# Halving the sixteen weights once, and picking a row's weight on GpSimd instead of ScalarE

## The reference, cut to what matters

```python
# x: (128 rows, 128 channels, 2048 steps); weights: (16, 128, 128)
W = weights[itok_B_0_15]                          # one of 16 matrices for each row
x = x + einsum('bct,bcd->bdt', x, W)              # stage 1, per row b
mask = arange(2048) < itok_B_8_3872[:, None]
u = x * mask[:, None, :]
k = S4D kernel of (log_dt, C, log_A_real, A_imag) # one filter of 2048 taps for each channel
y = irfft(rfft(u) * rfft(k))[..., :2048] + u * D  # causal convolution, per channel h
x = x + y * mask[:, None, :]                      # stage 2
```

## Time and profile before

| what | value |
|---|---|
| median of 3 runs | 2327.47 us (2319.9 to 2331.1) |
| the profiled execution | 2328.0 us, its span 2326.2 us |
| busy, share of the span | PE 93%, PEld 81%, DVE 71%, ACT 64%, POOL 51% |
| DMA | 716.26 MB, 308 GB/s over the span |
| granted TensorE clock | 0.993 of full speed |

### The profile page before, as it was taken

One profiled execution on the slowest core, in us unless ns is written; L12 is line 12 of the kernel. 1 busy time (PEld: TensorE's weight loads), 2 busy tenths in 40 slices (PEclk: granted clock), 3 DMA queues, 4 the chain that ended last, 5 costly groups with the idle time before them and its releaser, 6 DMA issues.

```text
span 2326.2 us, 61624 instructions
## 1 busy us (share of the span) xinstructions
PE 2169.9 (93%) x15101; PEld 1882.4 (81%) x15101; DVE 1652.8 (71%) x3359; ACT 1478.4 (64%) x4354; POOL 1175.6 (51%) x1862
## 2 busy tenths in 40 slices
PE   5777878999999999999999999999999999999999
PEld 2222226888888888888888888889999999999999
DVE  4999304777777777777777777667777777777776
ACT  4556556777777777777777677545555555555555
POOL 0995503666666666666666666433333333333332
PEclk9999999999999999999999999999999999999999
DMA  8999999999999999999999999889999899989997
GB/s 313 415 410 396 399 357 332 311 321 326 315 310 313 327 315 323 318 317 319 315 317 326 304 312 318 256 247 268 274 277 268 267 269 273 272 264 274 272 275 230
DMA packets 337444, 716.26 MB, mean 308 GB/s; under 512 B 39554, under 2 KB 170884, under 8 KB 337412
## 3 DMA queue, kind: packets, MB, share of 16 engines
q1 hardware_dynamic: 282116, 514.54, 72.5%
q10 hardware_dynamic: 55296, 201.35, 21.7%
HBM read 395.92 MB, written 319.82 MB: 308 GB/s over the span
## 4 chain that ended last, share of the span: by engine, by line
PE 52%; DMA 18%; SPq 8%; issue 7%; DVE 6%; ACT 5%; ACTq 5%; DVEq 0%
PE bank L907 11%; DMA toep<-k_scratch 11%; PE bank L908 10%; PE bank L909 10%; PE bank L952 6%; PE bank L944 6%; PE bank L889 5%; PE bank L876 3%; DMA row_x<-in_x 3%; SPq L339 3%; DVE decay L810 3%; SPq L355 2%; ACTq L522 2%; ACT row_y L547 2%; DMA decay<-x_scratch 2%
## 5 line engine op out<-in xcount | busy, mean ns | idle before, releaser
L798 DVE TENSOR_TENSOR u_lo<-bank,u_hi 128x512 fp32r<-128x512 f32 x512 | 352.2, 688 | 212.6 <-ACT u_hi L604 209.0
L907 PE MATMUL bank<-t_hi,u_hi 128*128 128x256 f32 x1024 | 361.8, 353 | 40.3 <-DMA toep<-k_scratch 39.4
L952 PE MATMUL bank<-toep,u_odd 128*128 128x128 f32 x2048 | 393.2, 273 | 0.0
L810 DVE COPY_PREDICATED decay<-mask,bank 128x512 f32<-128x512 uint8 x512 | 379.3, 741 | 14.0 <-PE bank L909 4.3
L547 ACT ACTIVATE row_y<-bank 128x512 f32<-128x512 f32 x512 | 301.6, 589 | 133.5 <-ACT row_y L547 47.5
L490 POOL TENSOR_TENSOR x_lo<-row_x,x_hi 128x256 fp32r<-128x256 f32 x496 | 371.5, 779 | 0.0
L804 DVE TENSOR_TENSOR s_lo<-state,s_hi 128x128 fp32r<-128x128 f32 x768 | 238.0, 310 | 163.5 <-ACT s_hi L616 160.5
L876 PE MATMUL bank<-row_x,w_sel 128*128 128x512 f32 x528 | 266.1, 631 | 90.9 <-DMA row_x<-in_x 51.3
L467 POOL TENSOR_TENSOR outer<-par 128x256 f32<-128x256 f32 x512 | 315.3, 637 | 20.5
L464 POOL COPY par<-table 128x71 f32 (+1 forms) x256 | 62.3, 243 | 514.1 <-PE bank L909 514.1
L613 ACT ACTIVATE state<-bank 128x128 f32<-128x128 f32 x768 | 211.4, 275 | 168.4 <-PE bank L909 150.5
(11 more groups left out here) (139 smaller groups left out, 5437.7 us busy)
## 6 DMA issues: line engine op xcount, KB each, us to landing
row_x<-in_x SPq DMA_DIRECT2D x256, 512.0 KB, 6.6
x_scratch<-row_y ACTq DMA_DIRECT2D x256, 512.0 KB, 5.7
decay<-x_scratch SPq DMA_DIRECT2D x256, 512.0 KB, 5.9
out<-decay SPq DMA_DIRECT2D x128, 512.0 KB, 4.7
out<-decay ACTq DMA_DIRECT2D x128, 512.0 KB, 5.6
b_scratch<-b_mat SPq DMA_DIRECT2D x128, 256.0 KB, 6.5
t_hi<-k_scratch SPq DMA_DIRECT2D x256, 128.0 KB, 4.8
t_lo<-k_scratch SPq DMA_DIRECT2D x256, 128.0 KB, 4.6
```

Source lines behind the costliest of these rows:

```text
L798: v.tensor_tensor(u_lo[j % 2][:, blocks, :], t_bank[q][:, :].rearrange("s (k b) -> s k b", b=B), u_hi[j % 2][:, blocks, :].bitcast(fp32), ...
L810: v.copy_predicated(tile[j][:, cols], mask[:, seg * SEG + q * BANK:seg * SEG + (q + 1) * BANK], y_bank[q][:, :]).then_inc(y_taken, 1)
L907: mm(to, w_hi, m_hi, start=start, stop=False, skip_group_check=True)
L952: mm(y[:, P:CHUNK], u_odd[i][:, c, :], toep[j][:, P - 1::-1], start=False, stop=True, skip_group_check=True)
```

## The change

The sixteen weights (already with the identity added) are rounded once, by one ScalarE instruction over 128x2048, into a new tensor `w_all_hi`, at the place where `halve_w` of row 0 stood. `halve_w` is gone from ScalarE. In `split_row` GpSimd reads the row's condition into a register, waits for the buffer (`row_made`), copies the chosen rounded half to `w_hi`, forms `w_lo` from `w_all` and `w_all_hi`, and only then waits for `x_hi`. ScalarE's wait for the buffer moves into `halve_x`. The row stage is as before.

```diff
+        w_all_hi = sb("w_all_hi", [P, NCOND, P], fp32r)
+        w_halved = sem("w_halved")
...
             def split_row(m, j):
 
-                i = j % 2
+                i, n = j % 2, m + ROWS_FIRST
+                which = pool.value_load(cond_sb[0:1, bass.ds(n, 1)], min_val=0, max_val=NCOND - 1)
+                pool.wait_ge(row_made, n * NQ - NQ)
+                whole, half = (a[:, bass.ds(which, 1), :].rearrange("c k d -> c (k d)") for a in (w_all, w_all_hi))
+                pool.tensor_copy(w_hi[i][:, :], half)
+                pool.tensor_tensor(w_lo[i][:, :], whole, half.bitcast(fp32), ALU.subtract)
                 pool.wait_ge(row_halved, m + 1)
-                pool.tensor_tensor(w_lo[i][:, :], w_sel[j][:, :], w_hi[i][:, :].bitcast(fp32), ALU.subtract)
...
+            pool.wait_ge(w_halved, 1)
             for m in range(2):
                 split_row(m, m)
...
                 if q == 0:
+                    act.wait_ge(row_made, n * NQ - NQ)
                     act.wait_ge(x_loaded[j], n * 4 + (16 - j * 4))
...
-            def halve_w(m, j):
-
-                n = m + ROWS_FIRST
-                which = act.value_load(cond_sb[0:1, bass.ds(n, 1)], min_val=0, max_val=NCOND - 1)
-                act.wait_ge(row_made, n * NQ - NQ)
-                w = w_all[:, bass.ds(which, 1), :].rearrange("c k d -> c (k d)")
-                nc.scalar.activation(w_sel[j][:, :], w, ACT.Copy)
-                nc.scalar.activation(w_hi[j % 2][:, :], w, ACT.Copy)
...
-            halve_w(0, 0)
+            nc.scalar.activation(w_all_hi[:, :, :], w_all[:, :, :], ACT.Copy).then_inc(w_halved, 1)
...
                     if next_row:
-                        halve_w(k + 1, j1)
                         halve_x(k + 1, j1, 0)
```

## The result

The changed kernel takes 2318.84 us in the median of 12 runs (2307.13 to 2324.89), against 2326.35 us of before in the same rounds: ratio 0.9964, 95% interval 0.9949 to 0.998. In a second series it took 2322.24 us, ratio 0.9974 (0.9954 to 0.9994). So it is faster by some 0.3%, and both intervals leave out 1. That is less than the 0.5% that the prediction took as the limit of what one can tell; the forecast was 2324.0.

A forecast was written before the change was run, and what follows sets the result against it. The bound was two interleaved channel loops, each of TensorE's body, issue and the late Toeplitz load's transfer. The sum was 2328.0 - 5 + 1 + 0 = 2324.0 us, own range 2318 to 2328, overall range 2312 to 2335.

The forecast's parts named there:

- ScalarE's late state costs TensorE, and the change ends it: Interleaved segment: TensorE's 0.31 us wait for state, 50 times, goes; at 0.2 us each, 10 us of body.
- The end of the body follows TensorE, so VectorE's part costs nothing: End of a channel: take_y comes 0.29 us after TensorE's last product, so VectorE's handover counts nothing; 9 us at most.
- rival B: The whole loop shortens, by 7.8 us and 9 us of VectorE's handover, to 2311 us; chance 0.12.
- A saving in the body is worth half: Two interleaved loops, even and odd channels: a microsecond saved in one body gives half; 10 us becomes 5 us.
- 1 us is given back: Interleaved segment: TensorE may find the other loop's channel ahead and earlier issues partly queue; 1 us of the 5 lost.
- GpSimd's work is hidden: Per row, GpSimd's added read, copy and subtraction, 0.9 + 0.3 + 0.46 = 1.7 us, fit into 3.16 us of idle time.
- Once: nothing: Before the first row, ScalarE's one-time 128x2048 rounding takes 2.2 us and costs 0, at most 0.5 us.
- Rival A: Nothing arrives: DMA engines at 0.96 absorb the earlier issues, each Toeplitz load lands when it did; 2328 us, chance 0.16.
- Rival C: Slower by collision: SyncE's earlier store of the filter's rows meets the Toeplitz loads in flight; 2338 us, chance 0.09.
- Rival D: GpSimd is late: a read over 2.7 us delays x_lo and par; at 3.7 us, 2390 us; chance 0.03.

The follow-up runs named there:

- e1: The kernel before the change, with Toeplitz tiles loaded for the first four channels only: 2270.49 us, ratio 0.976 to the kernel before.
- e2: The changed kernel with Toeplitz tiles loaded for the first four channels only: 2237.19 us, ratio 0.9615 to the kernel before.
- e5: The kernel before the change run once more, word for word the same: 2324.33 us, ratio 0.999.
- e9: The changed kernel with SyncE's store of the matrices moved behind the Toeplitz loads of the same channel: 2366.47 us, ratio 1.0183 to the kernel before.
- e3: The kernel before the change, with Toeplitz loads issued ahead of the x_scratch load and the store of the matrices: 2482.46 us, ratio 1.0666.
- e4: The changed kernel with Toeplitz loads issued ahead of the x_scratch load and the store of the matrices: 2473.16 us, ratio 1.0634 to the kernel before.
- e11: The kernel before the change, with the matrices' store moved behind the Toeplitz loads and the row load behind the filter's store: 2338.91 us, ratio 1.0062.
- e10: The changed kernel with the matrices' store moved behind the Toeplitz loads and the row load behind the filter's store: 2283.40 us, ratio 0.9829.
- e7: The kernel before the change, with row loads of 64 of the 128 channels in the interleaved segment: 2313.24 us, ratio 0.9935.

## Why the prediction was right, point by point

- **ScalarE's late state costs TensorE, and the change ends it.** Right, and shown by e1 and e2 with the wait in the rows. The size of a case was a little too small: I took 0.2 us of the visible 0.31. In the channels behind a gap under 8.35 us, where nearly all of these waits are, TensorE's part went from 7.59 and 7.57 us to 7.31 in both profiles, 0.27 each. Over all channels it shortened by 0.09 us, or 12 us in sum, where the prediction had 10.
- **The end of the body follows TensorE, so VectorE's part costs nothing.** Wrong. This was read off 0.29 us between the last product and `take_y` in one channel, and in that channel VectorE came straight from `e_lo`. The handover was 0.20 us in the mean, 0.26 behind a short gap, and it fell to 0.15. That is 0.05 us, 6 us in sum and 3 on the segment, a third of the whole saving. The prediction costed it at nothing and kept up to 9 us for the range and for rival B.
- **A saving in the body is worth half.** The pieces add up to two channels in all four profiles. The body's 0.14 us are 17 us in sum, and half of that is 8.6 us.
- **1 us is given back.** Too little. About 3.7 us were: 8.6 less the 4.9 by the `x_hi` rows. The place was named (TensorE still at the other loop's channel) and is seen as 0.17 us more after the landing. The two errors, 3.6 us too little saved and 2.7 too little given back, nearly cancel; 4 us net were forecast and 4.9 were found in the segment. That the total came so close is luck, all the more as the pairs of profiles differ by 3.5 to 4.9 us within themselves. By the medians the changed kernel is 7.5 us below the kernel before in the first series, and in the second 5.8 below the kernel before (2328.07) and 2.1 below e5.
- **GpSimd's work is hidden.** Right. The read took 0.68 us where 0.9 was allowed, partly while `e_mat` still ran, the copy 0.29 for 0.3, the subtraction 0.47 for 0.46. `x_lo` still waits 2.1 us, and 1.8 was said.
- **Once: nothing.** Right; 1.93 us for 2.2.
- **Rival A** (nothing arrives because the DMA engines are full) falls by the two ratios that leave out 1. Its condition holds while the Toeplitz loads are in flight (a share of 0.99), and some of the saving was given back. **Rival B** (the whole loop shortens, by 17 us) named `e_lo`, and this became short. Both of its parts came, and both smaller: 5.8 us from TensorE's part for its 7.8, 3 from the handover for its 9. VectorE's groups from 600 to 1400 us (busy us, mean ns), before and then after:

```profile
L804 DVE TENSOR_TENSOR s_lo<-state,s_hi 128x128 fp32r<-128x128 f32 x269 | 82.5, 307 | 102.6 <-ACT s_hi L616 102.4
L793 DVE TENSOR_TENSOR e_lo<-e_mat,e_hi 128x256 fp32r<-128x256 f32 x90 | 73.0, 811 | 0.0
L762 DVE TENSOR_TENSOR m_mat<-halves,par 128x128 f32<-128x128 f32 x89 | 63.1, 709 | 0.0
```
```profile
L802 DVE TENSOR_TENSOR s_lo<-state,s_hi 128x128 fp32r<-128x128 f32 x269 | 113.5, 422 | 112.3 <-ACT s_hi L615 106.7
...
L791 DVE TENSOR_TENSOR e_lo<-e_mat,e_hi 128x256 fp32r<-128x256 f32 x90 | 40.5, 449 | 0.0
...
L760 DVE TENSOR_TENSOR m_mat<-halves,par 128x128 f32<-128x128 f32 x90 | 25.1, 279 | 0.0
```

`e_lo` fell from 811 to 449 ns and `m_mat` from 709 to 279, `s_lo` rose from 307 to 422. The longest `e_lo` of the whole span took 875 ns before and 455 after. The second `take_y` waits 0.53 us for TensorE after the change, so most of VectorE's time went into its own idle time, and the 0.05 us of handover are what reached the loop. How much of that is `e_lo`'s and how much comes from the earlier `u_hi` was not separated. The Trainium skill ("SBUF — State Buffer", Who interferes with whom) lets exactly these instructions, with two SBUF inputs, block against GpSimd's reads of SBUF. By it `s_lo`, which GpSimd's copy and subtraction may now meet, should rise, and it did; that this is the cause of all three was not tested by itself.
- **Rival C** (the filter's store collides with the loads) had its condition misread: it took the store to start a few tenths after the load's landing, and in the kernel before it is issued 2.9 us ahead of that landing in every channel. It did start earlier, 5.4 us after the body's start instead of 5.8, and the landing did not get longer (4.88 to 4.74). **Rival D** fell by the 2.1 us that are left.

The point that I had not seen is the Toeplitz load's own dependence on the filter's store. It was 5.3 us of SyncE's waits and became the bound as soon as the load was moved (e9, and with the wait for `x_scratch` e3 and e4).

## What to carry to other kernels

When a wait ends on two engines by turns, price a saving by taking the covering wait away altogether: 33 us showed here where the kernel as it stood gave 5. Before calling an instruction bound by the engine that feeds it, look at what its own engine did just before: 0.29 us behind TensorE was VectorE's `e_lo`, not TensorE. Before moving a transfer up in a queue, look for what it waits for that has only just been in time; moving that one first turned a loss of 1.8% into a gain of 1.7%. And read a small gain from two profiles of each kernel, by the stretch that was changed: the untouched row stage alone moved its end by up to 10 us.

## What the runs showed of the hardware

- A register read from SBUF has no fixed price: 277 ns at the least on ScalarE, 568 in the median before, 1077 in e11 and up to 1481; on GpSimd 358 at the least and 682 in the median in the changed kernel, 930 in e10. The longer ones came in the kernels whose loads were reordered. What lengthens the read was not isolated; a Toeplitz load in flight is at most a part of it (954 ns without one, 1120 with one, in e11).
- GpSimd's sequencer reads the register while its engine still works on `e_mat`: a read of 0.68 us left only 45.7 / 116 = 0.39 us of idle time.
- One 128x2048 rounding on ScalarE took 1.93 us. Sixteen 128x128 ones would take 3.3 us, an estimate from the 0.41 us in the earlier trace rows from the start of `w_sel` to that of `x_hi`, with `w_sel` and `w_hi` in between (16 x 0.41 / 2).
- A load's time to landing did not fall with traffic issued behind it: 256 KB less of that in each channel left it at 4.9 us (e7). It was 2.8 to 3.4 us where 1.0 to 1.4 MB stood ahead of it (e3, e4, e9), 4.8 us with 1.7 MB, and 4.8 and 5.2 us with 2.1 MB (e11, e10). The amount ahead was not varied by itself.
